# Reordering the first loads of an RNN and LSTM kernel: input weights first, x over two queues, h0 behind the bias rows

## The chip, the cores and the metric

The kernel runs on one core of a Trainium2 chip. The time is the device time of one execution in microseconds (us), given as the median of several runs. Engines: TensorE (PE; its weight loads are listed as PEld), VectorE (DVE), ScalarE (ACT), GpSimd (POOL) and SyncE (SP), which here only issues transfers. ACT issues a few transfers too; "SPq" and "ACTq" are the two engines' issuing instructions, and in the views of the DMA queues q1 is the queue of SP and q10 that of ACT.

## The reference

An RNN layer and an LSTM layer, each with a residual, over x of 32 sequences, 128 steps and 512 features, all float32:

```python
# x: (32, 128, 512); cond_1024: (32, 512); L0: Wx, Wh (512, 512), b (512); L1: Wx, Wh (512, 2048), b (2048)
def rnn(x, h0, Wx, Wh, b):
    xW = einsum('ntd,dh->nth', x, Wx) + b
    h = h0
    for t: h = tanh(h @ Wh + xW[:, t]);  h_t[:, t] = h
def lstm(x, h0, Wx, Wh, b):
    c = 0; h = h0
    for t: a = (x @ Wx + b)[:, t] + h @ Wh
           i, f, o = sigmoid(a[:, 0:H]), sigmoid(a[:, H:2H]), sigmoid(a[:, 2H:3H]);  g = tanh(a[:, 3H:])
           c = f * c + i * g;  h = o * tanh(c);  h_t[:, t] = h
x = x + rnn(x, cond_1024, ...)
x = x + lstm(x, cond_1024, ...)
```

## The kernel before

The kernel is one program with a hand-written stream for each engine, ordered by semaphores. A global step k runs from 0 to T + 6 (T = 128): at k the RNN does its step k and the LSTM its step k - 7. The hidden state of 32 sequences by 512 units lies on 128 partitions as four quarters of 32 (`quarter(j)`, j the block of 128 units). x comes in groups of four time steps (`TG`): `load_x` (L418) fetches one group by four transfers of 64 KB, one for each quarter j, all adding to one semaphore. Every 512 bytes of it is a separate row in memory.

All weights are fetched whole and stay on the chip: WxR and WhR (`wxr_raw`, `whr_raw`, 1 MB each), WhL and WxL (`whl_raw`, `wxl_raw`, four chunks of 1 MB each). The names `in_L_cond_Wx` and so on of the trace stand for both layers. SP issues x's group 0, WxR, WhR and then the chunks (L429 to L440); the helper `load_chunk` (L425) issues a chunk only when an earlier load has landed: the first chunk of WhL behind WxR, the second behind WhR, each later one behind the chunk two before it. ACT issues h0 and the two biases at its start (L603 to L606), then loads its function table (L610, by way of a small sigmoid).

What the first step needs, engine by engine:

- PE (from L1474): six warming matmuls on the identity (`fill`, L1470); the RNN bias spread to all partitions by a small product (L1479), which needs the bias rows `bias_rows_r` (they are landed in `pre_r`); the same into the two RNN banks (L1482); the LSTM bias product (L1484), which needs `bias_rows_l` (landed in `pre_l`); six more fills, which wait for ACT's copy of the RNN bias (`bias_done`, L614); `product_r(0)` (L1393), x times WxR; two fills; `recurrent_r(0)` (L1404), h0 times WhR.
- DVE (from L1154): `turn_x(0)` (L906), the transposition of x's group 0, which waits for its four quarters; `start_state` (L895, L896), two transpositions of h0, one for each layer; `rnn_weight_peak` (L1047), the largest absolute value of WxR; then `rnn_turn(0)` (L1152), the transposition of the first new state, which waits for ACT's tanh (L810).
- ACT: the bias copy (L614), tanh of step 0 (L810), and then `bias_of_l` (L618) and the peak of WhR (L729) before tanh of step 1.

```python
            for k in range(END):
                ...
                if k == 0:
                    fill(ps_pk, 2)
                if k < LAG:
                    recurrent_r(k)
```

Of the kernel before, what the change touches and what calls it, by code (L numbers as in the profile page):

```python
# [13 lines left out]
TG = 4  # L14
DMA = 16
# [26 lines left out]
def rnn_lstm_kernel(nc, x, h0, WxR, WhR, bR, WxL, WhL, bL, out):  # L42
    B, T, D = x.shape
    H = WhR.shape[0]
    J = H // P
# [7 lines left out]
    with ctx:  # L53
        def sb(name, shape, dt=F32):
            return ctx.enter_context(nc.sbuf_tensor(name, shape, dt))
# [4 lines left out]
        def sem(name):  # L60
            return ctx.enter_context(nc.semaphore(name))
# [20 lines left out]
        h0n = sb("h0n", [P, P])  # L82
# [84 lines left out]
        s_h0 = sem("h0_loaded")  # L167
# [201 lines left out]
        def wait(eng, s, value):  # L369
            if value > 0:  # L370
                eng.wait_ge(s, value)
# [15 lines left out]
        def sliced_dram(t, first):  # L387
            v = t.rearrange("b t (j u) -> j b t u", j=J)
            return [v[j, :, first:first + TG, :] for j in range(J)]

        def chunk_rows(w, k):
            return w.rearrange("(p k) n -> k p n", k=J)[k]
# [5 lines left out]
        def quarter(j):  # L398
            return slice(j * B, (j + 1) * B)
# [11 lines left out]
        def store_last(eng, j):  # L411

            done = stored if j < 2 else stored_by_act
            eng.dma_start(sliced_dram(out, T - TG)[j][:, TG - 1, :], xb[(NG - 1) % NX][quarter(j), TG - 1, :]).then_inc(done, DMA)

        block = ctx.enter_context(nc.Block())

        def load_x(eng, g):  # L418
            for j, src in enumerate(sliced_dram(x, g * TG)):
                eng.dma_start(xb[g % NX][quarter(j), :, :], src).then_inc(x_in[g % NX], DMA)  # L420

        @block.sync
        def _(sp):

            def load_chunk(dst, w, k, loaded, behind):  # L425
                sp.wait_ge(behind, DMA)
                sp.dma_start(dst, chunk_rows(w, k)).then_inc(loaded, DMA)

            load_x(sp, 0)  # L429
            sp.dma_start(wr_raw[OF_X][:, :], WxR.rearrange("(p k) n -> p (k n)", k=J)).then_inc(s_wr[OF_X], DMA)  # L430
            sp.dma_start(wr_raw[OF_H][:, :], WhR.rearrange("(p k) n -> p (k n)", k=J)).then_inc(s_wr[OF_H], DMA)
            load_chunk(whl_raw[0][:, :], WhL, 0, s_whl[0], s_wr[OF_X])
            load_chunk(whl_raw[1][:, :], WhL, 1, s_whl[1], s_wr[OF_H])
            load_x(sp, 1)
            load_chunk(whl_raw[2][:, :], WhL, 2, s_whl[2], s_whl[0])
            load_chunk(whl_raw[3][:, :], WhL, 3, s_whl[3], s_whl[1])
            load_chunk(wxl_raw[0][:, :], WxL, 0, s_wxl[0], s_whl[2])
            load_chunk(wxl_raw[1][:, :], WxL, 1, s_wxl[1], s_whl[3])
            load_chunk(wxl_raw[2][:, :], WxL, 2, s_wxl[2], s_wxl[0])
            load_chunk(wxl_raw[3][:, :], WxL, 3, s_wxl[3], s_wxl[1])  # L440
            load_x(sp, 2)
            sp.wait_ge(s_wxl[2], DMA)
            load_x(sp, 3)
            for g in range(4, NX):
                load_x(sp, g)
            def peaks_to_row(i):
                first, count = BATCHES[i]
                sp.wait_ge(x_peaked, first + count - G1)
                if i == BY_PRODUCT:
                    sp.wait_ge(t_split, 8)  # L450
                wait(sp, row_reduced, i - BY_PRODUCT)
                sp.dma_start(peak_row,
                             peaks[:, X_PEAK + first:X_PEAK + first + count]).then_inc(row_loaded, DMA)

            def peaks_to_all(i):
                n = i - BY_PRODUCT
                sp.wait_ge(row_reduced, n + 1)
                wait(sp, scale_step, X_STEPS * (i - 1) + 1 if n > 0 else 0)
                sp.dma_start(peak_wide, peak_largest.unsqueeze(1).broadcast_to([1, P, 4])).then_inc(wide_loaded, DMA)

            for g in range(NG - 1):

                if g in EXCHANGE_BEHIND:
                    peaks_to_row(EXCHANGE_BEHIND[g])
                    peaks_to_all(EXCHANGE_BEHIND[g])
                sp.wait_ge(out_done, TG * (g + 1))
                for j, dst in enumerate(sliced_dram(out, g * TG)):
                    sp.dma_start(dst, xb[g % NX][quarter(j), :, :]).then_inc(stored, DMA)
                if g + NX < NG:
                    sp.wait_ge(stored, DMA * J * (g + 1))  # L470
                    load_x(sp, g + NX)

            sp.wait_ge(out_done, T - 1)
            for j, dst in enumerate(sliced_dram(out, T - TG)):
                sp.dma_start(dst[:, 0:TG - 1, :], xb[(NG - 1) % NX][quarter(j), 0:TG - 1, :]).then_inc(stored, DMA)
            sp.wait_ge(out_done, T)
            for j in (0, 1):
                store_last(sp, j)
            sp.wait_ge(stored, DMA * (J * (NG + 1) - 2))
            sp.wait_ge(stored_by_act, 2 * DMA)  # L480
# [119 lines left out]

        @block.scalar
        def _(act):
            act.dma_start(h0n[:, :], h0.rearrange("b (j u) -> j b u", j=J)).then_inc(s_h0, DMA)  # L603
            act.dma_start(bias_rows_r, bR.rearrange("(j u) -> j u", j=J)).then_inc(s_bias_r, DMA)
            act.dma_start(bias_rows_l.rearrange("j (g u) -> j g u", g=G),
                          bL.rearrange("(g j u) -> j g u", g=G, j=J)).then_inc(s_bias_l, DMA)  # L606


            act.wait_ge(ones_done, 1)
# [277 lines left out]
        def _(dve):  # L887
# [162 lines left out]
            def rnn_weight_low(of):  # L1050
                dve.wait_ge(r_high[of], 3)
                for (dst, src), (high, _) in zip(r_parts(wr[of][1], wr_raw[of]), r_parts(wr[of][0], wr_raw[of])):
                    nc.vector.scalar_tensor_tensor(out=dst, in0=src, scalar=r_scale[:, of:of + 1],
                                                   in1=high, op0=ALU.mult, op1=ALU.subtract).then_inc(r_split, 1)
# [533 lines left out]
```

## Time and profile before

| | us |
|---|---|
| median of 3 runs | 849.19 |
| the runs | 849.07 to 853.11 |
| span of the profiled execution | 847.5 |
| PE busy | 830.7 (98%) |
| DVE busy | 660.3 (78%) |
| ACT busy | 582.7 (69%) |
| POOL busy | 337.6 (40%) |

The page gives for the profiled execution its span, from the first to the last instruction; its own time is not shown apart from that, and the median of the runs is 1.7 above the span. The busy time of PE is modelled from the starts of pipelined matmuls. The chain of waits is followed back from the last instruction: each piece is what the next was released by. In the views in order of time, rows that are alike are merged, and the bracket at a row's end is the idle time ahead of it on its engine and what ended it.

### The profile page before, as it was taken

The numbers are of one execution on the slowest core, as the hardware profiler recorded it, in microseconds if no ns is written. First come the engines' busy times: TensorE is split into PE (matmuls) and PEld (weight loads), VectorE is DVE, ScalarE is ACT, GpSimd is POOL, SyncE is SP. The second block draws the span as 40 slices with busy tenths as digits, with TensorE's granted clock in tenths as the row PEclk, the third lists the DMA queues.
The fourth block names the chain that finished last, engine by engine and source line by source line (L and its number), as shares of the span: only waits on it lengthen the run. The fifth ranks groups of instructions, "written<-read, shape, count | busy, mean of one in ns | idle before, by whom it ended". The sixth has DMA issues, their size and how long they took to land.

```text
span 847.5 us, 52211 instructions
## 1 busy us (share of the span) xinstructions
PE 830.7 (98%) x22860; PEld 621.8 (73%) x22860; DVE 660.3 (78%) x1830; ACT 582.7 (69%) x1596; POOL 337.6 (40%) x697
## 2 busy tenths in 40 slices
PE   7999999999999999999999999999999999999996
PEld 4665556687777877777777787777777777777885
DVE  3579688788887877888778887888878887777765
ACT  4896477777676777766767776676777677677642
POOL 1212466834334343443444434344343443434320
PEclk9999999999999999999999999999999999999999
DMA  8801100111001111100111100011110000000000
GB/s 319 267 19 27 29 15 16 28 29 29 17 17 30 29 29 29 29 10 23 29 29 29 29 21 20 22 29 29 29 28 17 17 17 17 17 15 17 16 15 18
DMA packets 40196, 30.71 MB, mean 36 GB/s; under 512 B 5772, under 2 KB 38688, under 8 KB 38688
## 3 DMA queue, kind: packets, MB, share of 16 engines
q1 hardware_dynamic: 39712, 27.27, 11.2%
q8 instruction: 179, 2.93, 1.5%
q14 instruction: 49, 0.40, 0.2%
q10 hardware_dynamic: 256, 0.11, 0.0%
HBM read 18.95 MB, written 8.39 MB: 32 GB/s over the span
## 4 chain that ended last, share of the span: by engine, by line
PE 93%; DVE 3%; ACT 2%; DMA 1%; issue 1%; SPq 0%; ACTq 0%; DVEq 0%
PE ps_l L1279 35%; PE ps_l L1345 28%; PE ps_r L1422 9%; PE ps_r L1442 9%; PE ps_l L1323 4%; PE ps_l L1292 2%; PE ps_l L1312 2%; PE ps_r L1404 1%; PE ps_r L1393 1%; DMA whr_raw<-in_L_cond_Wh 1%; PE ps_l L1238 1%; DVE pre_l L1080 0%; PE ps_l L1266 0%; ACT gates L795 0%; PE ps_l L1256 0%
## 5 line engine op out<-in xcount | busy, mean ns | idle before, releaser
L496 POOL TENSOR_TENSOR xb<-xb,h_l 128x128 f32<-128x128 f32 x127 | 58.0, 457 | 420.3 <-DVE h_lo L1126 414.2
L1345 PE MATMUL ps_l<-whl_raw,wxl_raw 128*32 128x256 f16 x3888 | 125.2, 273 | 1.7 <-ACT wxl_raw L700 1.3
L1345 PE MATMUL ps_l<-wxl_hi,wxl_raw 128*32 128x256 f16 x2592 | 124.6, 273 | 0.0
L1279 PE MATMUL ps_l<-whl_hi,hT_hi 128*32 128x512 f16 x1888 | 123.5, 379 | 1.1 <-DVE hT_hi L1110 1.1
L1279 PE MATMUL ps_l<-whl_hi,hT_lo 128*32 128x512 f16 x1888 | 123.3, 379 | 0.0
L1279 PE MATMUL ps_l<-whl_lo,hT_hi 128*32 128x512 f16 x1888 | 123.3, 379 | 0.0
L1345 PEld LDWEIGHTS ps_l<-whl_raw,wxl_raw 128*32 128x32 f16 x3888 | 104.0, 97 | 15.8 <-ACT ps_l L681 2.7
L795 ACT ACTIVATE gates<-pre_l 128x256 f32<-128x256 f32 x108 | 45.1, 417 | 101.5 <-DVE pre_l L1080 101.5
L1279 PEld LDWEIGHTS ps_l<-whl_hi,hT_lo 128*32 128x32 f16 x1888 | 51.9, 97 | 50.3
L1279 PEld LDWEIGHTS ps_l<-whl_lo,hT_hi 128*32 128x32 f16 x1888 | 51.9, 97 | 50.3
L1080 DVE SCALAR_TENSOR_TENSOR pre_l<-ps_l,g_products,wxl_raw 128x256 f32<-128x256 f32 x108 | 47.5, 480 | 48.3 <-PE ps_l L1279 43.6
L1080 DVE SCALAR_TENSOR_TENSOR pre_l<-ps_l,g_products,bias_l 128x256 f32<-128x256 f32 x108 | 47.5, 480 | 47.1 <-PE ps_l L1279 40.9
L533 POOL TENSOR_TENSOR whr_raw<-whr_raw 128x64 f32<-128x64 f32 x216 | 80.5, 393 | 4.2
L1345 PEld LDWEIGHTS ps_l<-wxl_hi,wxl_raw 128*32 128x32 f16 x2592 | 70.8, 97 | 12.0
L810 ACT ACTIVATE h_r<-pre_r 128x128 f32<-128x128 f32 x114 | 35.4, 310 | 63.8 <-DVE pre_r L1137 63.8
L1345 PE MATMUL ps_l<-wxl_lo,wxl_raw 128*32 128x256 f16 x1296 | 73.8, 273 | 0.0
L1279 PEld LDWEIGHTS ps_l<-whl_hi,hT_hi 128*32 128x32 f16 x1888 | 51.5, 97 | 27.3 <-DVE hT_hi L1110 1.4
L1152 DVE STREAM_TRANSPOSE hT_r<-h_r 128x128 f32<-128x128 f32 x128 | 52.7, 412 | 18.8 <-ACT h_r L810 18.7
L565 POOL TENSOR_TENSOR whr_raw<-xT,hT_r 128x128 f32<-128x128 f32 x108 | 50.0, 463 | 27.6 <-DVE hT_r L1152 27.6
L802 ACT ACTIVATE tanh_c<-c 128x128 f32<-128x128 f32 x128 | 39.5, 309 | 30.9 <-DVE c L1095 25.7
L747 ACT ACTIVATE xr<-ps_r,g_products 64x128 f32<-64x128 f32 x114 | 41.5, 364 | 26.4 <-PE ps_r L1422 21.6
L505 POOL TENSOR_TENSOR xb<-xb,h_r 128x128 f32<-128x128 f32 x128 | 59.4, 464 | 0.0
(178 smaller groups left out, 1936.4 us busy)
## 6 DMA issues: line engine op xcount, KB each, us to landing
xb<-in_x SPq DMA_DIRECT2D x128, 64.0 KB, 2.2
out<-xb SPq DMA_DIRECT2D x124, 64.0 KB, 1.8
whl_raw<-in_L_cond_Wh SPq DMA_DIRECT2D x4, 1024.0 KB, 6.4
wxl_raw<-in_L_cond_Wx SPq DMA_DIRECT2D x4, 1024.0 KB, 5.9
wxr_raw<-in_L_cond_Wx SPq DMA_DIRECT2D x1, 1024.0 KB, 5.6
whr_raw<-in_L_cond_Wh SPq DMA_DIRECT2D x1, 1024.0 KB, 7.7
out<-xb SPq DMA_DIRECT2D x4, 48.0 KB, 1.6
wxl_raw<-peaks SPq DMA_DIRECT2D x5, 2.0 KB, 1.9
```

Of the source, the lines that this page charges most:

```text
L496: nc.gpsimd.tensor_tensor(xb[g % NX][:, t, :], xb[g % NX][:, t, :], h_l[s % 2][:, :], ALU.add).then_inc(out_done, 1)
L505: nc.gpsimd.tensor_tensor(xb[g % NX][:, t, :], xb[g % NX][:, t, :], h_r[r % 2][:, :], ALU.add).then_inc(y_done, 1)
L533: nc.gpsimd.tensor_tensor(y[:, out, :, :], y[:, a, :, :], y[:, b, :, :], op).then_inc(y_blocks, 1)
L565: nc.gpsimd.tensor_tensor(yA[g % 2][:, first:first + 2, :, t // 2, :], xT[g % 2][:, :, t, :].rearrange("p (a k) b -> p a k b", a=2), hT_r[ ...
L747: nc.scalar.activation(xr[r % 2][0:64, :], ps_r[r % 2][64:128, P:2 * P], ACT.Copy, scale=unscale_r[64:128, g:g + 1])
L795: nc.scalar.activation(gates[:, 0:2 * P], pre_l[:, 0:2 * P], ACT.Sigmoid).then_inc(lstm_act, 1)
L1080: nc.vector.scalar_tensor_tensor(out=pre_l[:, half * HALF:(half + 1) * HALF], in0=gates_psum(s, half), scalar=unscale_l(s), in1=added[half ...
L1152: nc.vector.transpose(hT_r[:, :, :], by_chunk(h_r[r % 2][:, :])).then_inc(rnn_hT, 1)
L1279: last = nc.tensor.matmul(ps_l[s % 4][quarter(j), :], (hT_hi, hT_lo)[h_part][:, k, :], gate_slice(whl[w_part][k], j), start=False, stop=(h ...
L1345: last = nc.tensor.matmul(at[quarter(j), :], stationary, weights[:, j, :, :], start=False, stop=(y_part == 1 and k == 1), skip_group_check ...
L1422: last = nc.tensor.matmul(ps_r[r % 2][quarter(2 * p + c), 0:2 * P], (hT_r_hi, hT_r_lo)[h_part][:, 2 * p + k, :], quadrant_of_r16(wr[OF_H][ ...
L1442: last = nc.tensor.matmul(ps_r[r % 2][quarter(2 * p + c), 0:2 * P], x16[x_part][g % 2][:, 2 * p + k, t * B:(t + 1) * B], quadrant_of_r16(w ...
```

## The change

`load_x` gets an argument for the quarters it loads. SP's first transfer is WxR, then the quarters 2 and 3 of x's group 0, then WhR. ACT's first transfers are quarters 0 and 1, then the RNN bias rows, the LSTM bias rows, and h0. Nothing else differs; the line numbers of the new kernel are one higher behind L419 or two behind L603.

```diff
-        def load_x(eng, g):
-            for j, src in enumerate(sliced_dram(x, g * TG)):
+        def load_x(eng, g, quarters=range(J)):
+            for j in quarters:
+                src = sliced_dram(x, g * TG)[j]
                 eng.dma_start(xb[g % NX][quarter(j), :, :], src).then_inc(x_in[g % NX], DMA)
...
-            load_x(sp, 0)
             sp.dma_start(wr_raw[OF_X][:, :], WxR.rearrange("(p k) n -> p (k n)", k=J)).then_inc(s_wr[OF_X], DMA)
+            load_x(sp, 0, (2, 3))
             sp.dma_start(wr_raw[OF_H][:, :], WhR.rearrange("(p k) n -> p (k n)", k=J)).then_inc(s_wr[OF_H], DMA)
...
-            act.dma_start(h0n[:, :], h0.rearrange("b (j u) -> j b u", j=J)).then_inc(s_h0, DMA)
+            load_x(act, 0, (0, 1))
             act.dma_start(bias_rows_r, bR.rearrange("(j u) -> j u", j=J)).then_inc(s_bias_r, DMA)
             act.dma_start(bias_rows_l.rearrange("j (g u) -> j g u", g=G),
                           bL.rearrange("(g j u) -> j g u", g=G, j=J)).then_inc(s_bias_l, DMA)
+            act.dma_start(h0n[:, :], h0.rearrange("b (j u) -> j b u", j=J)).then_inc(s_h0, DMA)
```

SP's stream from its start, before (`wxr_raw` and `whr_raw` are WxR and WhR, `xb` is x):

```order
1 L420 DMA xb<-in_x 32x4x128 x4
2 L430 DMA wxr_raw<-in_L_cond_Wx 128x2048
3 L431 DMA whr_raw<-in_L_cond_Wh 128x2048
4 L427 DMA whl_raw<-in_L_cond_Wh 128x2048 [waits wxr_loaded]
5 L427 DMA whl_raw<-in_L_cond_Wh 128x2048 [waits whr_loaded]
```

and after the change:

```order
1 L430 DMA wxr_raw<-in_L_cond_Wx 128x2048
2 L421 DMA xb<-in_x 32x4x128 x2
3 L432 DMA whr_raw<-in_L_cond_Wh 128x2048
4 L428 DMA whl_raw<-in_L_cond_Wh 128x2048 [waits wxr_loaded]
5 L428 DMA whl_raw<-in_L_cond_Wh 128x2048 [waits whr_loaded]
```

WxR has moved ahead of x, and two of x's four quarters are gone from SP. ACT's stream from its start, before (`h0n` is h0, `pre_r` and `pre_l` are where the bias rows land):

```order
1 L603 DMA h0n<-in_cond 128x1x128
2 L604 DMA pre_r<-in_L_cond_b 4x128
3 L605 DMA pre_l<-in_L_cond_b 4x4x128
4 L610 ACT_TABLE_LOAD
5 L610 ACTIVATE table_first<-ones 128x1
```

and after the change:

```order
1 L421 DMA xb<-in_x 32x4x128 x2
2 L605 DMA pre_r<-in_L_cond_b 4x128
3 L606 DMA pre_l<-in_L_cond_b 4x4x128
4 L608 DMA h0n<-in_cond 128x1x128
5 L612 ACT_TABLE_LOAD
6 L612 ACTIVATE table_first<-ones 128x1
```

Two transfers of x stand ahead of the bias rows, h0 behind them, and the table load has two more issues in front of it less h0's earlier place.

## Rows read from the trace of the kernel before

**Rows 1.** The page: span, busy time of each engine, and the chain by engine.

```profile
span 847.5 us, 52211 instructions
...
PE 830.7 (98%) x22860; PEld 621.8 (73%) x22860; DVE 660.3 (78%) x1830; ACT 582.7 (69%) x1596; POOL 337.6 (40%) x697
...
PE 93%; DVE 3%; ACT 2%; DMA 1%; issue 1%; SPq 0%; ACTq 0%; DVEq 0%
```

**Rows 2.** The chain in order of time, 0 to 60 us: start us, us, what.

```profile
0.74 0.38 SPq L420
...
1.18 0.42 SPq L420
...
2.67 0.49 SPq L430
...
3.21 7.66 DMA whr_raw<-in_L_cond_Wh
...
10.91 1.12 PE ps_r L1404 x32
...
17.01 0.68 issue
...
23.30 0.77 issue
```

**Rows 3.** Rows in order of time, PE, 0 to 12 us: start, us, what [idle before].

```profile
1.52 2.74 PE L1470 MATMUL ps_l<-ident 128*128 128x512 f16 x6 [1.52 <-POOL ident L486]
...
4.65 0.46 PE L1479 MATMUL ps_l<-pre_r,gates 4*128 4x128 f32 x2 [0.39 <-DMA pre_r<-in_L_cond_b]
...
5.48 1.12 PE L1484 MATMUL ps_l<-pre_l,gates 4*128 4x512 f32 x2
...
6.54 1.47 PE L1470 MATMUL ps_l<-ident 128*128 128x512 f16 x6
...
8.31 1.08 PE L1393 MATMUL ps_r<-wxr_raw,xT 128*32 128x128 f32 x32 [0.31 <-DMA wxr_raw<-in_L_cond_Wx]
...
9.33 0.60 PE L1470 MATMUL ps_pk<-ident 128*128 128x512 f16 x2
...
10.91 1.08 PE L1404 MATMUL ps_r<-whr_raw,hT_r 128*32 128x128 f32 x32 [0.98 <-DMA whr_raw<-in_L_cond_Wh]
```

**Rows 4.** Rows in order of time, DVE, 5 to 13 us.

```profile
5.80 1.08 DVE L906 STREAM_TRANSPOSE xT<-xb 128x512 f32<-128x512 f32 x1 [3.98 <-DMA xb<-in_x]
...
6.82 0.35 DVE L895 STREAM_TRANSPOSE hT_r<-h0n 128x128 f32<-128x128 f32 x1
7.11 0.36 DVE L896 STREAM_TRANSPOSE h0T<-h0n 128x128 f32<-128x128 f32 x1
...
8.29 2.29 DVE L1047 TENSOR_REDUCE peaks<-wxr_raw 128x1 f32<-128x2048 f32 x1 [0.83 <-DMA wxr_raw<-in_L_cond_Wx]
...
12.37 0.42 DVE L1152 STREAM_TRANSPOSE hT_r<-h_r 128x128 f32<-128x128 f32 x1 [1.79 <-ACT h_r L810]
```

**Rows 5.** DMA issues of 0.7 to 1 us and of 0 to 4.4 us, last number us to landing.

```profile
xb<-in_x SPq DMA_DIRECT2D x1, 64.0 KB, 1.9
...
wxr_raw<-in_L_cond_Wx SPq DMA_DIRECT2D x1, 1024.0 KB, 5.6
```

**Rows 6.** Rows in order of time, ACT, 0 to 5 us.

```profile
0.75 1.17 ACTq L603 DMA_DIRECT2D h0n<-in_cond  x1
1.95 0.31 ACTq L604 DMA_DIRECT2D pre_r<-in_L_cond_b  x1
2.30 0.29 ACTq L605 DMA_DIRECT2D pre_l<-in_L_cond_b  x1
2.62 1.28 ACT L610 ACT_TABLE_LOAD   x1 [2.62 <-issue]
3.92 0.20 ACT L610 ACTIVATE table_first<-ones 128x1 f32<-128x1 f32 x1
```

**Rows 7.** DMA queues, 2.18 to 2.5 us, then 6 to 9 us: packets, MB, engines' share.

```profile
q1 hardware_dynamic: 42, 0.02, 20.6%
q10 hardware_dynamic: 29, 0.01, 15.2%
...
DMA packets 170, 1.26 MB, mean 421 GB/s; under 512 B 16, under 2 KB 16, under 8 KB 16
...
q1 hardware_dynamic: 170, 1.26, 100.3%
```

**Rows 8.** The last two WxL chunks: issue, the last one's landing time, its first weight load.

```profile
27.32 2.79 SPq L427 DMA_DIRECT2D wxl_raw<-in_L_cond_Wx  x2
...
wxl_raw<-in_L_cond_Wx SPq DMA_DIRECT2D x1, 1024.0 KB, 5.6
...
36.73 0.14 PEld L1246 LDWEIGHTS ps_l<-wxl_raw,yT 128*32 128x32 f32 x4
```

**Rows 9.** By stage: busy (x) of PE, PEld, DVE, ACT, POOL; granted clock, DMA share, GB/s.

```profile
0.00:4.30 4.30, 2.74 (x6) 0.73 (x6) 0.49 (x2) 1.49 (x2) 0.99 (x8) 1.00 0.41 96
```

## The prediction

> **What bounds the kernel now.** I read the page first: the span, the engines' shares and the chain that ended last [rows 1]. The reader should see that TensorE (PE) is busy 98% of the span and holds 93% of the chain; no operation of PE, VectorE (DVE), ScalarE (ACT) or GpSimd is changed here. Only the opening is touched, where the chain has 1% of DMA. So I read the chain in order of time next [rows 2]. It starts with SyncE issuing four quarters of the first x (0.74 to 2.63), then WxR (wxr_raw, 2.67), then WhR (whr_raw, 3.21), waits 7.66 us for WhR, and lets `recurrent_r(0)` start at 10.91. Call that start R. Behind R the chain in order of time has only PE, ACT, DVE and "issue" pieces, no DMA; the later weight loads have cover (below). So a microsecond won or lost at R is one at the end, if nothing else gives way.
>
> Third, what else must be there before R. PE's own rows in order of time [rows 3]: fills that need only the identity (1.52 to 4.26); the RNN bias product (4.65), started by the landing of the bias rows; the two ps_r products; the LSTM bias product (5.48 to 6.60); six fills (to 8.01); `product_r(0)` at 8.31, started by WxR; two fills (9.33 to 9.93); then 0.98 us of waiting for WhR. Two lengths follow: from the bias row's landing to the end of the six fills 8.01 - 4.65 = 3.36, and from `product_r(0)` to the end of the last fills 9.93 - 8.31 = 1.62. With B for the landing of bias_rows_r and no other wait, R cannot come before B + 4.98. With B at 4.65 that is 9.63: **PE's opening has 1.28 us of slack today.** DVE's rows [rows 4]: `turn_x(0)` at 5.80 when x has landed (1.08), `start_state` (0.35 and 0.36), then the peak of WxR (2.29, to 10.58), and `rnn_turn(0)` at 12.37, 1.46 behind R. It has 1.8 us of slack.
>
> **The change, part by part.**
>
> *WxR first on SyncE.* Its issue moves from 2.67 to 0.74. The trace has no WxR with nothing ahead of it. Upper end: today's 5.6 us from issue to landing [rows 5], so 6.3. Lower end: the first x quarter lands 1.9 us after its issue [rows 5], and one more megabyte costs the distance of the landings of WxR (PE started on it at 8.31) and WhR (10.91) [rows 3], 2.6 us: 0.74 + 1.9 + 2.6 = 5.2. I take the middle, 5.8. That no longer matters to `product_r(0)`, if PE's fills end later than that.
>
> *WhR's issue.* Two x issues fewer ahead of it, 0.38 and 0.42 [rows 2], with their gaps of 0.05: from 3.21 to about 2.3. Upper end with its 7.66: 9.95. Lower end: 2.6 behind WxR's 5.2, 7.8; with 0.5 for the two x quarters in between (four issues a step of 0.48, [rows 2]) 8.3. From the middle, 5.8 + 2.6 + 0.5 = 8.9. So **WhR comes 0.9 to 2.6 us earlier, and stops being what R waits for.** The chunks of WhL and WxL, each issued by the landing two before, come earlier with it; nothing in the chain waited for them, so I cost that at nothing. The cover: the second-last WxL chunks land before PE asks, and the last, issued last in the stretch that ends at 30.11 and 5.6 to landing, so there by 35.7, is a microsecond ahead of its weight load at 36.73 [rows 8].
>
> *Two x quarters on ACT ahead of the bias rows.* This is the price. ACT's issues now: h0 1.17, bias 0.31, bias 0.29 [rows 6]. I take the 1.17 for whatever comes first on ACT and 0.38 to 0.51 for a second x; the RNN bias is then issued at about 0.75 + 1.17 + 0.45 = 2.4 and not at 1.95. Lower end for B: the same 2.7 us from issue to landing as now (1.95 to 4.65) and 0.35 for the shortest extra issue, 5.0. The upper end comes from what stands ahead. An x quarter is 128 rows of 512 bytes, 8 for each of the 16 DMA engines; ACT's queue had one such transfer (h0) before the bias rows and now has two, and beside them SyncE's queue holds no longer other small rows but WxR. In the stretch where weights alone move, 154 packets over 512 bytes take 48.1 engine-microseconds (1.003 x 16 x 3), 0.31 each, carrying 8 KB [rows 7]. If the two queues take turns on an engine, each of ACT's first 8 small packets waits for one of WxR's 8, and the bias rows come behind the second x right after WxR: 5.2 to 6.3 plus up to 0.5 for a quarter, so 6.8 at the top. The trace has no row of small beside large packets to choose by; I take WxR's middle and 0.2 for the small rows behind it, which is also about the middle of the two ends: **B = 6.0.** Then R = 6.0 + 4.98 = 10.98 against 10.91: **+0.1 us.** With the ends, R is 10.0 (-0.9) to 11.8 (+0.9); WhR at 9.95 at the worst is under all of it.
>
> The Trainium skill, page "DMA: Bandwidth & Descriptors", section "Queues, rings and completion order", says that each DMA engine goes round its queues a packet at a time; that rule speaks against this change. The only mixing the trace shows, small with small (q1 and q10 both moving, [rows 7]), does not contradict it; no row here has small beside large. By strict turns the sum is the +0.1 above, with ACT's small rows passing freely it is -0.9. The same page, section "Issuing engines are not separate DMA queues", says that a second issuing engine saves only issue time; by that alone the gain is the 0.9 of WhR's issue.
>
> *The ACT table load* follows the last issue: from 2.62 it moves by two x issues less the reordered h0, about 0.9, to end with its first use at about 5.0 instead of 4.12 [rows 6]. The bias copy needs PE, at B + 0.5 = 6.5; hidden. If that cover were gone it would cost the difference, under 0.5.
>
> *h0 behind the bias rows.* Issued about 3.1 instead of 0.75. DVE needs it for hT_r. It takes turns with WhR's packets, so I put it at 9.2, between WhR's 8.9 and its 9.95. hT_r is then there at 9.6, under R. Behind it on DVE stand h0T (0.36) and the WxR peak (2.29), 9.2 + 0.35 + 0.36 + 2.29 = 12.2, against `rnn_turn(0)` wanted at 10.98 + 1.46 = 12.44. Cover 0.2; cost nothing.
>
> *x itself:* `turn_x(0)` ends before 8.5 even if x lands 1.5 later than at 5.8; PE wants it at B + 3.36 = 9.4. Nothing.
>
> **Sum:** +0.1 us. The profiled execution's span is 847.5; 847.5 + 0.1 = 847.6, and with the 1.7 by which the median of the runs (849.19) stands above that span, **849.3**. I call anything within 0.5% (4.2 us) no change, about what a measurement of this kernel can tell. Even the whole 1.28 of slack is a third of that.
>
> **The rivals.**
>
> 1. *The bias rows get through at once* (B = 5.0): R = 10.0, limited equally by B and WhR's upper end: 0.9 faster, 848.3. For it: a 512-byte packet is short, and the bias rows are few. Against: today's bias landing already takes 2.7 us behind one h0.
>
> 2. *h0 is what comes last.* Its 128 small rows take turns with WhR and WhL; at the worst it lands where WhR does now, 10.87. DVE then runs h0's two transposes and the WxR peak until 10.87 + 3.0 = 13.9 and `rnn_turn(0)` comes 1.5 late, the first step's recurrence behind it: 850.7. The point from which it decides is a landing after 9.4. For it: the cover I found is 0.2. Against: WhR's bytes should be through by then.
>
> 3. *PE's clock.* The six fills before 4.26 take 2.74 us, the six before 8.01 take 1.47 [rows 3], though the granted-clock column says 1.00 [rows 9]; by the durations PE was at first at the lower of its two levels (1.2 and 2.4 GHz) and later at the higher. The new wait before the bias product is 1.7 us and not 0.39. If that sets the level back, the fills cost 1.27 more and `product_r(0)` up to 1: about +2.3, 851.6. Against: the 0.98 of waiting before R did it no harm, the matmuls after it take as long as those ahead (1.08 for 32).
>
> 4. *It doesn't do what it says:* WxR's first bytes come no earlier because WxR shares with x from two queues, and all landings stay. Then R is held by WhR or B near where it is: no change, 849.2.
>
> **How the numbers follow.** Forecast (with rival 4, which gives the same time) 0.52; bias rows early 0.25; h0 late 0.18; clock 0.05. The cases span 848.3 to 851.6. One of the three runs was at 853.11, 3.9 above the median, so a median of few runs can stray upwards by more than the mechanism. The range leaves the clock case and the strays partly out: 847.5 to 851.6, the low end 0.8 under the fastest case because earlier weight chunks may shorten one of the two unexplained PE pauses (0.68 and 0.77, [rows 2]). None of the cases reaches 0.5%; only strays do: faster 0.02, same 0.94, slower 0.04.
>
> **What would show it.** SyncE: WxR issued at 0.74, WhR near 2.3. `product_r(0)` not started by a DMA but straight behind the fills, near 9.4. The wait before `recurrent_r(0)` gone or tiny, with R within 0.9 of 10.9. The bias product starting at 5.0 to 6.8 and named as waiting for pre_r; PE's idle time moved from in front of WhR to in front of the bias product. `rnn_turn(0)` started by ACT's h_r, not by DVE's own queue. The forecast is wrong if R moves by over 1 us, if a DMA again stands in front of R, or if R moves and the end does not follow it one for one.

## The result and the profile after

| | median, us | runs | lowest to highest |
|---|---|---|---|
| before | 850.22 | 22 | 849.00 to 853.11 |
| changed | 851.60 | 22 | 850.83 to 852.63 |

The ratio is 1.0016 with a 95% interval of 1.0008 to 1.0023: the changed kernel is 1.4 us slower, 0.16%, which is no change by the 0.5% of the prediction, and it is clear of the noise. The kernel before has spread out with more runs: its median is 1.0 above the one the prediction started from. A second series of the changed kernel (e12 below) gave 1.0014 (1.0003 to 1.0024).

The page of the changed kernel, span and chain by engine, against [rows 1]. The span is 1.9 us longer, and ACT's share of the chain has gone from 2% to 3%:

```profile
span 849.5 us, 52211 instructions
...
PE 93%; ACT 3%; DVE 2%; issue 1%; DMA 1%; ACTq 0%; DVEq 0%
```

The chain in order of time, 0 to 40 us (start, us, what), against [rows 2]. It no longer starts with SyncE and WhR but with ACT's queue and the RNN bias rows:

```profile
0.73 0.42 ACTq L421
...
1.67 5.26 DMA pre_r<-in_L_cond_b
```

PE's rows in order of time, against [rows 3]:

```profile
1.52 2.74 PE L1472 MATMUL ps_l<-ident 128*128 128x512 f16 x6 [1.52 <-POOL ident L487]
...
7.06 0.76 PE L1481 MATMUL ps_l<-pre_r,gates 4*128 4x128 f32 x2 [2.79 <-DMA pre_r<-in_L_cond_b]
...
8.47 1.91 PE L1486 MATMUL ps_l<-pre_l,gates 4*128 4x512 f32 x2
...
10.31 2.74 PE L1472 MATMUL ps_l<-ident 128*128 128x512 f16 x6
...
12.98 1.94 PE L1395 MATMUL ps_r<-wxr_raw,xT 128*32 128x128 f32 x32
...
14.85 1.03 PE L1472 MATMUL ps_pk<-ident 128*128 128x512 f16 x2
...
15.81 1.08 PE L1406 MATMUL ps_r<-whr_raw,hT_r 128*32 128x128 f32 x32
```

Two things are to be seen. The bias product starts at 7.06 and not at 4.65, after 2.79 us of waiting. And from there each group takes longer than it did: the six fills 2.74 instead of 1.47, `product_r(0)` 1.94 instead of 1.08, the two fills 1.03 instead of 0.60. These are the durations of the first fills at 1.52: PE works at the lower of its two levels (1.2 and 2.4 GHz) until just before `recurrent_r(0)`, which takes 1.08 as before. From the start of the bias product to R it is 8.75 us, and before it was 6.26, with 0.31 of waiting for WxR and 0.98 for WhR in it. R is at 15.81, **4.9 us later than before** (one profile of each kernel; a second profile of the changed kernel, e12, has R at 15.14).

DVE's rows, against [rows 4]:

```profile
7.26 1.08 DVE L908 STREAM_TRANSPOSE xT<-xb 128x512 f32<-128x512 f32 x1 [5.44 <-DMA xb<-in_x]
...
10.70 0.41 DVE L897 STREAM_TRANSPOSE hT_r<-h0n 128x128 f32<-128x128 f32 x1 [2.35 <-DMA h0n<-in_cond]
...
11.31 2.24 DVE L1049 TENSOR_REDUCE peaks<-wxr_raw 128x1 f32<-128x2048 f32 x1
```

x, h0 and the peak are all done by 13.6, ahead of R. The issues of SyncE and ACT, and the DMA issues with their time to landing, against [rows 5, 6]:

```profile
0.73 0.90 ACTq L421 DMA_DIRECT2D xb<-in_x  x2
0.74 0.39 SPq L430 DMA_DIRECT2D wxr_raw<-in_L_cond_Wx  x1
...
1.67 0.58 ACTq L605 DMA_DIRECT2D pre_r<-in_L_cond_b  x1
2.12 0.67 SPq L432 DMA_DIRECT2D whr_raw<-in_L_cond_Wh  x1
```

```profile
wxr_raw<-in_L_cond_Wx SPq DMA_DIRECT2D x1, 1024.0 KB, 5.5
whr_raw<-in_L_cond_Wh SPq DMA_DIRECT2D x1, 1024.0 KB, 7.7
```

The weights did what the change wanted: WxR landed at 6.2 and not 8.3, WhR at 9.8 and not 10.9. The RNN bias was issued earlier than before (1.67 against 1.95) and landed 2.3 later.

The DMA queues of the changed kernel from 3.0 to 3.5 and from 4.0 to 4.5 us show why:

```profile
DMA packets 41, 0.19 MB, mean 380 GB/s; under 512 B 0, under 2 KB 19, under 8 KB 19
...
q1 hardware_dynamic: 22, 0.18, 85.3%
q10 hardware_dynamic: 19, 0.01, 6.4%
...
q1 hardware_dynamic: 26, 0.21, 100.4%
q10 hardware_dynamic: 24, 0.01, 8.1%
```

22 packets of 8 KB on SyncE's queue beside 19 small ones on ACT's, then 26 beside 24: by these counts the two queues take turns about one for one in this profile (e3 and e1 below look otherwise). Before, from 2.18 to 2.5 us, ACT's queue moved 29 small packets in a third of a microsecond beside small ones [rows 7]; beside large ones it moves 24 in a half. By the Trainium skill, page "DMA: Bandwidth & Descriptors", section "Queues, rings and completion order", each DMA engine goes round its queues a packet at a time; this trace agrees, with the 19 beside 22 and 24 beside 26 above.

### The profile page after: what moved, and what is told of

It is laid out like the page before. It is cut to its first block, busy times and chain, and to the rows that moved or that the text cites. A ratio compares the mean times of both kernels' runs of the same rounds, so it can differ in the third digit from the quotient of the medians.

```text
span 849.5 us, 52211 instructions
## 1 busy us (share of the span) xinstructions
PE 832.7 (98%) x22860; PEld 621.1 (73%) x22860; DVE 661.0 (78%) x1830; ACT 582.0 (69%) x1596; POOL 339.0 (40%) x697
## 4 chain that ended last, share of the span: by engine, by line
PE 93%; ACT 3%; DVE 2%; issue 1%; DMA 1%; ACTq 0%; DVEq 0%
PE ps_l L1281 35%; PE ps_l L1347 28%; PE ps_r L1424 9%; PE ps_r L1444 9%; PE ps_l L1325 4%; PE ps_l L1294 2%; PE ps_l L1314 2%; PE ps_r L1395 1%; ACT whl_lo L714 1%; PE ps_r L1406 1%; DMA pre_r<-in_L_cond_b 1%; DVE pre_l L1082 0%; PE ps_l L1268 0%; PE ps_l L1258 0%; PE ps_l L1248 0%
## 5 line engine op out<-in xcount | busy, mean ns | idle before, releaser
L1347 PEld LDWEIGHTS ps_l<-whl_raw,wxl_raw 128*32 128x32 f16 x3888 | 104.0, 97 | 15.8 <-ACT ps_l L683 2.7
L506 POOL TENSOR_TENSOR xb<-xb,h_r 128x128 f32<-128x128 f32 x128 | 61.4, 480 | 0.0
```

The costliest lines, as they stand in the source:

```text
L506: nc.gpsimd.tensor_tensor(xb[g % NX][:, t, :], xb[g % NX][:, t, :], h_r[r % 2][:, :], ALU.add).then_inc(y_done, 1)
L1347: last = nc.tensor.matmul(at[quarter(j), :], stationary, weights[:, j, :, :], start=False, stop=(y_part == 1 and k == 1), skip_group_check ...
```

## The experiments

Two theories stood after this reading. **A:** the bias rows are late because they queue behind x on ACT beside WxR, PE has nothing to do for 2.8 us, and then works at its lower level. **B:** h0, which landed at 10.7 as rival 2 feared, would cost as much by itself. Each run has one profile, of one of its executions, while the ratios come from all of them. The experiments also had to say how 4.9 us at R became 1.4 to 1.9 at the end.

### e1: bias rows first on ACT

```diff
-            load_x(act, 0, (0, 1))
             act.dma_start(bias_rows_r, ...)
             act.dma_start(bias_rows_l..., ...)
+            load_x(act, 0, (0, 1))
             act.dma_start(h0n[:, :], ...)
```

> The change, with ACT's issues in the order bias rows, x quarters 0 and 1, h0. Theory A (the bias rows are late because they queue behind x beside WxR, PE idles 2.8 us and then works at its lower level until recurrent_r(0)): the bias rows land before 4.7, the second six fills take 1.47 and not 2.74, recurrent_r(0) starts at 10 to 11.3, and the end is 0 to 0.9 us under the kernel before. Theory B (h0's late landing, 10.7, is what costs): h0 is still behind two x quarters, so recurrent_r(0) still waits until 11.1 or later, DVE's queue (h0T, the peak of WxR to about 13.5) holds rnn_turn(0), and the end is 1 to 1.5 us over the kernel before.

852.08 against 849.87, ratio 1.0015 (1.0004 to 1.0025): nothing gained on the changed kernel. The RNN bias product started straight behind the first fills, but its rows show the lower level still, and the LSTM bias rows came only at 5.96 (order of time, PE and DVE):

```profile
4.19 0.79 PE L1481 MATMUL ps_l<-pre_r,gates 4*128 4x128 f32 x2
...
5.96 2.07 PE L1486 MATMUL ps_l<-pre_l,gates 4*128 4x512 f32 x2
...
7.96 2.74 PE L1472 MATMUL ps_l<-ident 128*128 128x512 f16 x6
9.17 1.09 DVE L908 STREAM_TRANSPOSE xT<-xb 128x512 f32<-128x512 f32 x1 [7.34 <-DMA xb<-in_x]
```

Theory A in its simple form falls: in this profile an early RNN bias did not by itself bring the higher level. x, now behind the bias rows, landed at 9.2, later than in the changed kernel. From 2 to 5 us ACT's queue moved no packet at all, though its x quarters were issued from 1.64 on; SyncE's moved 126. R was 13.46.

### e2: the change with more fills

```diff
             fill(ps_l[3], 3)
             fill(ps_l[0], 3)
+            fill(ps_l[3], 11)
             pe.wait_ge(spread_j_done, 1)
```

> The change, with 11 more fills on PE before the bias product (not needed for the result), so that PE works from 1.5 to about 7 us. It takes the idle stretch away and leaves the late landing. Theory A splits here: if the level of PE's clock is the larger part, the second six fills take 1.47 again, recurrent_r(0) starts 5.0 behind the bias rows' landing, at about 12 and not 15.8, and the end is within 0.5 us of the kernel before. If the idle stretch is not what sets the level back, the fills still take 2.74 and nothing moves. Theory B: recurrent_r(0) is at 12 as well, but rnn_turn(0) waits for DVE until 13.6, and the end stays 1 us or more over.

849.43 against 849.87, ratio 0.9997 (0.9988 to 1.0005). Adding 11 matmuls whose result is not used took away all that the change had cost. PE's rows:

```profile
1.52 6.78 PE L1472 MATMUL ps_l<-ident 128*128 128x512 f16 x17 [1.52 <-POOL ident L487]
...
8.23 0.48 PE L1482 MATMUL ps_l<-pre_r,gates 4*128 4x128 f32 x2
...
9.96 1.47 PE L1472 MATMUL ps_l<-ident 128*128 128x512 f16 x6
...
12.91 1.08 PE L1406 MATMUL ps_r<-whr_raw,hT_r 128*32 128x128 f32 x32
```

The second fills take 1.47 again, and from the bias product to R it is 12.91 - 8.23 = 4.68 us and not 8.75: **the level costs 4.1 us of the opening.** (In e12's profile of the changed kernel the same stretch is 7.97, and the cost 3.3.) In this profile R is still 2.0 later than before, h0 is as late as in the changed kernel (its transposition at 10.87), and yet the median is not later. The profiled execution itself is the slowest of e2's eleven, 851.25, with a span of 849.4; PE waits 0.99 us for a late WxL chunk in it. So its rows speak of the opening and not of the typical end. Theory B falls: h0's landing is hidden here, with 0.6 us of cover (DVE was done with the peak at 13.7 and `rnn_turn(0)` came at 14.36, released by ACT).

### e3: WxR first alone

```diff
-            load_x(sp, 0)
             sp.dma_start(wr_raw[OF_X][:, :], WxR...)
+            load_x(sp, 0)
             sp.dma_start(wr_raw[OF_H][:, :], WhR...)
```

(against the kernel before; ACT's issues are untouched).

> One part of the change alone: SyncE issues WxR, then all four x quarters, then WhR; ACT issues h0 and the bias rows as before. Taking turns: h0's eight small packets an engine wait for WxR's eight, so the bias rows, behind them, land at 5.5 to 6.5 although ACT's queue is as before; PE idles 1.3 to 2.2 us before the bias product. Rival (ACT's small packets pass freely and only the second x transfer ahead of the bias rows delays them): the bias rows land at 4.6 as before and recurrent_r(0) starts near 10.

852.84 (5 runs) against 849.87, ratio 1.0035 (1.0022 to 1.0049), the worst of the orders. ACT's queue is as before, with h0 alone ahead of the bias rows, and still they landed 4 us later than before:

```profile
8.61 0.76 PE L1480 MATMUL ps_l<-pre_r,gates 4*128 4x128 f32 x2 [4.35 <-DMA pre_r<-in_L_cond_b]
```

So WxR at the head of SyncE's queue is enough to delay them, without a second x transfer on ACT. But it is not done by turns here. From 2 to 5 us the only queue with packets is SyncE's, although h0 was issued on ACT at 0.74:

```profile
DMA packets 140, 0.93 MB, mean 309 GB/s; under 512 B 8, under 2 KB 28, under 8 KB 28
...
q1 hardware_dynamic: 140, 0.93, 77.4%
```

ACT's queue moved its first packet just before 5.1 us, when 126 of WxR's 128 had gone. The same holds in e1. Why its rows got turns from 2.5 us on in the changed kernel and none in these two is not shown. By stages, this run also shows the level itself; columns are the stretch, its length, busy (x) of PE, PEld, DVE, ACT and POOL, granted clock, DMA share and GB/s:

```profile
7.00:10.00 3.00, 1.39 (x6) 1.42 (x7) 0.94 (x1) 0.28 (x1) 0.00 (x0) 0.72 1.02 344
10.00:13.00 3.00, 3.00 (x7) 0.79 (x6) 2.89 (x4) 0.00 (x0) 0.00 (x0) 0.50 0.94 333
13.00:16.00 3.00, 3.00 (x37) 1.45 (x36) 0.00 (x0) 0.00 (x0) 0.00 (x0) 0.65 1.00 356
```

0.50 is the 1.2 GHz level. PE did nothing from 4.26 to 8.61; the clock fell in the stretch from 7 to 10 and was back by 16.

### e4: small rows first

```diff
-            sp.dma_start(wr_raw[OF_X][:, :], WxR...)
             load_x(sp, 0, (2, 3))
+            sp.dma_start(wr_raw[OF_X][:, :], WxR...)
...
-            load_x(act, 0, (0, 1))
             act.dma_start(bias_rows_r, ...)
             act.dma_start(bias_rows_l..., ...)
+            load_x(act, 0, (0, 1))
             act.dma_start(h0n[:, :], ...)
```

> SyncE issues x quarters 2 and 3, then WxR, WhR; ACT the bias rows, x quarters 0 and 1, h0. x is still split over two queues, but no large packet is ahead of it. By taking turns: the bias rows land at about 3.5, WxR is issued about 0.9 earlier than before and WhR lands at about 10, recurrent_r(0) starts at 9.9 to 10.2, 0.7 to 1 us earlier than before, if h0 (behind x on ACT, beside WxR) lands before 9. The end is 0.3 to 1 us under the kernel before. Rival: the opening is absorbed further on by ACT's queue (which runs without a gap from the first tanh), and the end does not move by more than 0.3.

850.18 against 849.87, ratio 1.0004 (0.9993 to 1.0014). R did not come earlier but at 12.99: two x quarters on ACT behind the bias rows met WxR after all, and PE waited 3.19 us for x:

```profile
10.86 1.24 PE L1395 MATMUL ps_r<-wxr_raw,xT 128*32 128x128 f32 x32 [3.19 <-DVE xT L908]
```

The wait cost more than its length: the products behind it fell back to the lower level, and `recurrent_r(0)` took 1.94 instead of 1.08. Although R was 2.1 later than before, the first cell of the LSTM (tanh_c of step 7) was 0.2 later, and the end within the noise.

### e5: x over two queues, then WxR

```diff
-            sp.dma_start(wr_raw[OF_X][:, :], WxR...)
             load_x(sp, 0, (2, 3))
+            sp.dma_start(wr_raw[OF_X][:, :], WxR...)
```

(ACT as in the change).

> The change with WxR put back behind x on SyncE (x quarters 2 and 3, WxR, WhR; ACT as changed: x quarters 0 and 1, bias rows, h0). All of x travels with small rows only. Expected by taking turns: x landed by 4.5, the bias rows at 4.2 to 5.2 (only the last of them meet WxR's first packets), WhR about 10, no long idle stretch of PE, recurrent_r(0) at 10 to 10.5. If a start R that is 0.5 to 0.9 earlier is worth as much at the end, the kernel is 0.5 to 0.9 us faster than before; if the opening has play behind it (e4: R 2.1 late, step 7 only 0.2 late), 0 to 0.3.

851.62 (6 runs) against 849.34, ratio 1.0026 (1.0012 to 1.0040). x landed by 4.4, the RNN bias by 4.2 and WhR at 9.8, as expected. But the LSTM bias product began only at 7.18, after 1.3 us of idle PE, and PE was at the lower level before that wait and stayed there (the RNN bias products took 0.79 and 1.06, the six fills from 9.18 to 11.92); R was 14.49. So the idle stretch, R and the end came out wrong: even this order leaves the LSTM bias rows beside WxR, and the opening is lost to the level.

### e6: h0 behind the bias rows, alone

```diff
-            act.dma_start(h0n[:, :], ...)
             act.dma_start(bias_rows_r, ...)
             act.dma_start(bias_rows_l..., ...)
+            act.dma_start(h0n[:, :], ...)
```

(the kernel before otherwise).

> The third part of the change alone: the kernel before with h0 issued behind the bias rows on ACT. The bias rows land near 3 to 4 instead of 4.65, the bias products start right behind the first fills at 4.2, h0 lands by 6 to 8 beside WxR, WhR at 10.9 still sets recurrent_r(0): no change (within 0.5 us). Rival: PE's waits move (a longer one before product_r(0)), the clock level comes later or falls in some runs, and the median is 0.5 us or more over.

849.85 against 849.34, ratio 1.0012 (1.0002 to 1.0022): 0.5 to 1.0 over, the rival's side. In its profile PE was again at the lower level until 12 (R 12.55), and this without any wait: from 1.52 to 12.0 it was never idle.

```profile
7.48 2.74 PE L1471 MATMUL ps_l<-ident 128*128 128x512 f16 x6
10.15 1.94 PE L1394 MATMUL ps_r<-wxr_raw,xT 128*32 128x128 f32 x32
```

So an opening without a gap is no guarantee of the higher level. The weights were late too. WxR landed at 10.0 and not 8.3, and PE waited twice for a WxL chunk, for which the prediction had counted on a microsecond of cover:

```profile
35.58 1.07 PE L1247 MATMUL ps_l<-wxl_raw,yT 128*32 128x512 f32 x8 [1.50 <-DMA wxl_raw<-in_L_cond_Wx]
...
38.94 1.07 PE L1247 MATMUL ps_l<-wxl_raw,yT 128*32 128x512 f32 x8 [0.57 <-DMA wxl_raw<-in_L_cond_Wx]
```

### e7 and e8: only R late

```diff
                 if k == 0:
-                    fill(ps_pk, 2)
+                    fill(ps_pk, 16)
```

(29 in e8; the kernel before otherwise).

> The kernel before with 14 more fills (0.22 us each, not needed for the result) just ahead of recurrent_r(0): loads and clock as before, R later by 9.93 + 3.05 - 10.91 = about 2.1 us. If R counts one for one, the end is 2.1 later. If there is play of 2.7 us between R and step 7 (as in the changed kernel, where 4.9 at R became 2.2), the end does not move.

> The same with 27 more fills: R at 9.93 + 5.9 = 15.8, as late as in the changed kernel, but with the loads of the kernel before and PE at its higher level. If lateness of R is all that the change costs, the end is 1.4 to 2.2 us later, as in the changed kernel; if the changed order of the loads costs something by itself, it is less than that; if R counts one for one, 4.9.

e7: 852.84 against 849.34, ratio 1.0053 (1.0037 to 1.0068); e8: 854.58, 1.0063 (1.0051 to 1.0075). R was not where I had set it in either profile: loads and program are those of the kernel before up to the fills, and still the opening was partly (e8) or wholly (e7) at the lower level. The kernel before can therefore have a slow opening as well; its one profile, with R at 10.91, shows a good one. e7's six runs reach from 851.25 to 856.45, and its profile is the slowest of them:

```profile
16.01 1.08 PE L1404 MATMUL ps_r<-whr_raw,hT_r 128*32 128x128 f32 x32
...
23.35 0.66 PE L1404 MATMUL ps_r<-whr_raw,hT_r 128*32 128x128 f32 x8 [1.68 <-issue]
48.40 0.31 ACT L802 ACTIVATE tanh_c<-c 128x128 f32<-128x128 f32 x1 [0.56 <-DVE c L1095]
```

R is as late as in the changed kernel (5.1 against 4.9 later than before), with the loads in their old order, and the first cell is 6.9 later: more than R, not less. A pause of PE of 1.68 us that waits for nothing on record stands in between. e8's profile, order of time and then by stage:

```profile
6.38 1.55 PE L1470 MATMUL ps_l<-ident 128*128 128x512 f16 x6
8.74 1.94 PE L1393 MATMUL ps_r<-wxr_raw,xT 128*32 128x128 f32 x32 [0.81 <-DMA wxr_raw<-in_L_cond_Wx]
10.61 8.32 PE L1470 MATMUL ps_pk<-ident 128*128 128x512 f16 x29
18.86 1.08 PE L1404 MATMUL ps_r<-whr_raw,hT_r 128*32 128x128 f32 x32
```

```profile
7.60:7.80 0.20, 0.20 (x2) 0.00 (x0) 0.00 (x0) 0.00 (x0) 0.00 (x0) 0.60 1.18 492
```

The clock rose for the first products and was lost again between 7.6 and 7.8, while PE was still in its fills. The wait of 0.81 us for WxR came behind the fall and cannot have caused it; the idle time ahead of it is 0.42 us before 4.69. R was 18.86, 7.95 later than before, and the first cell 5.23 later (below): 2.7 us fewer between R and the first cell, the same as in the changed kernel, with the loads in their old order. So e8 lost 2.7 us of R's lateness on the way and e7 added 1.8 to it; neither sum belongs to the change. In the runs of e8 the end is 5.2 later, as its first cell says.

The start of tanh_c of step 7 in the kernel before, the changed kernel, e2 and e8:

```profile
41.50 0.31 ACT L802 ACTIVATE tanh_c<-c 128x128 f32<-128x128 f32 x1 [0.56 <-DVE c L1095]
```

```profile
43.69 0.31 ACT L804 ACTIVATE tanh_c<-c 128x128 f32<-128x128 f32 x1 [0.56 <-DVE c L1097]
```

```profile
41.90 0.31 ACT L804 ACTIVATE tanh_c<-c 128x128 f32<-128x128 f32 x1 [0.56 <-DVE c L1097]
```

```profile
46.73 0.31 ACT L802 ACTIVATE tanh_c<-c 128x128 f32<-128x128 f32 x1 [0.56 <-DVE c L1095]
```

### e9 to e12: the same fills elsewhere, and the change once more

e9 is the kernel before with e2's line, e10 is e1 with it, e11 is e5 with it; e12 is the changed kernel unaltered.

```diff
             fill(ps_l[0], 3)
+            fill(ps_l[3], 11)
```

> The kernel before with the same 11 more fills on PE ahead of the bias product. Its loads are as before. PE works from 1.5 to about 6.7 us, so its clock should be at the higher level by the bias product in every execution; recurrent_r(0) comes at about 11.7 instead of 10.9, which the play behind it should swallow. If the level in the opening is also what spreads the runs of the kernel before, its median falls by 0.3 to 0.8 us and few runs stand above 851. Rival: the spread has another cause (a late weight chunk), and median and spread stay.

> The order of e1 (bias rows ahead of the x quarters on ACT, WxR first on SyncE) with the 11 more fills. If e1's 1.3 us over was the clock level, it comes down to the kernel before or up to 0.5 under it; if it was x's and h0's late landing, it stays 1 us or more over.

> The order of e5 (x over two queues, then WxR) with the 11 more fills. As e10: level theory, from 2.2 over down to the kernel before or up to 0.5 under it; a late LSTM bias landing (7.2 in e5) alone would leave 0.5 or more over.

> The changed kernel once more, beside the others on one chip: 1.0 to 2.2 us over the kernel before, no run under 850.5.

| | median (before 849.88) | ratio, 95% interval | the same order without the fills |
|---|---|---|---|
| e9 | 850.35 | 1.0009 (0.9998 to 1.0020) | 1 |
| e10 | 849.99 | 1.0008 (0.9998 to 1.0018) | e1: 1.0015 (1.0004 to 1.0025) |
| e11 | 849.86 | 0.9997 (0.9989 to 1.0006) | e5: 1.0026 (1.0012 to 1.0040) |
| e12 | 851.36 | 1.0014 (1.0003 to 1.0024) | |

e12 repeats the change's loss. e11 gives back all of e5's, and its interval does not meet e5's; e10's gain on e1 is within the intervals. e9 fell for the rival: with the clock at its higher level (in its profile) the kernel before is no faster, and its runs still reach from 848.10 to 852.97. So the opening's level is not what spreads the runs of the kernel before, or not alone. A late weight chunk is another source: PE waits 1.0 to 2.1 us in all for WxL in the profiles of e2, e6 and e9, and there the span ends 807.4 to 807.8 us behind the first cell; in the other eleven profiles it is 805.6 to 806.4. No run here sets its share. No version beats the kernel before: e2 and e11 equal it, and the intervals of e4, e9 and e10 reach it.

e12's profile has the fall of the clock on record, which the first profile of the changed kernel has not:

```profile
4.30:7.00 2.70, 0.00 (x0) 0.00 (x0) 0.00 (x0) 0.43 (x2) 0.00 (x0) 1.00 1.09 370
7.00:10.00 3.00, 2.83 (x9) 1.17 (x10) 1.10 (x1) 0.28 (x1) 0.00 (x0) 0.71 1.05 385
```

Here PE was idle from 4.26 to 7.17, the RNN bias product behind the wait still ran at the higher level (0.46), and the clock fell between 8.1 and 8.4, a microsecond after PE had gone back to work. In the first profile of the changed kernel the same product takes 0.76: there the level was already low behind the wait. The six fills take 2.74 in both.

## Why the prediction was right, and where it was not

The measured 851.60 lies at the very top of the range, and the likeliest case, +0.1, did not happen. The case that did, the clock, I had given 0.05; that its 851.6 is the measured figure is luck, as its parts show below. By the prediction's own signs it failed: R moved by 4.9 us and not by less than 1, and the end did not follow one for one. Point by point:

- **The bound.** R waited for WhR before, and PE's opening had 1.28 us of slack: right, and the changed chain starts where the slack ran out, at the bias rows.
- **WxR and WhR.** 5.8 and 8.9 in the sum; 6.2 and 9.8 measured, inside both pairs of ends. WhR stopped being what R waits for, as said.
- **The bias rows.** B = 6.0 with a top of 6.8; PE started on them at 7.06, after a wait to 6.92. The mechanism, turns one for one with WxR, fits this profile, though e1 and e3 show that it is no rule. Two terms were short: WxR landed at 6.2 and not 5.8, and the bias rows 0.7 behind it, where I had 0.2. By 5.0 us ACT's queue had moved 109 of its 256 packets of x; the second quarter and the bias rows came after WxR, with the small rows of both queues.
- **ACT's issues.** I took 1.17 us for the first transfer whatever it was. x's first took 0.42 [a row of the chain above]; the 1.17 belonged to h0 coming first. A small error to the good.
- **PE's clock (rival 3).** This is the step that failed. I priced it at 2.3 us in all and gave it 0.05, because 0.98 us of waiting before R had done no harm. It cost 4.1 us in the opening (e2), as every group from the bias product on ran at the lower level. The two groups that I had priced, the six fills and `product_r(0)`, cost 1.27 and 0.86, near my 2.3; the bias products cost 1.52 and the last two fills 0.42, which I had at nothing. And the level need not be "set back" by the wait: in the first profile of the changed kernel it had not risen when the bias product came.
- **R counts one for one at the end.** Wrong, and it saved the range. R went up by 4.9, the first cell by 2.19, the last cell's tanh by 1.94, the median by 1.4. The 2.7 us between R and step 7 went in steps: `rnn_turn(2)` was still 4.90 late, `rnn_turn(3)` 4.16, `rnn_turn(4)` 3.40. That is two steps of about 0.75, at the two pauses of PE of 0.68 and 0.77 in [rows 2], which the changed kernel's profile does not have. A third, on PE's weight loads, stands a little further on in the kernel before:

```profile
30.22 0.14 PEld L1238 LDWEIGHTS ps_l<-whl_raw,h0T 128*32 128x32 f32 x3 [1.04 <-issue]
```

  and in the changed kernel the same eight matmuls run through without it (32.24, 1.09 us). 0.68, 0.77 and 1.04 are 2.5 of the 2.7. Lateness alone does not take these pauses away. From R to the first cell it is 27.9 us in the changed kernel, e3 and e8, where PE has no such pause; 30.6 in the kernel before; and 32.4 in e7, with R at 16.0. PE pauses for nothing on record in seven of the fourteen profiles, among them e1 (1.5), e5 (1.5 and 0.5) and e7 (1.7), whose R is 2.5 to 5.1 later than before. So the 2.7 is a difference between two single executions, and the 4.9 is one too: e7 shows that the old order of loads can have the low level as well. What the medians say is the 1.4.

  What the pauses are is open. In the kernel before, the queue that the page calls "instruction" moves one packet at 15.2, 21.4 and 27.7 us, each 1.5 to 1.9 us ahead of a pause (in e7 at 21.0, the pause beginning at 21.7). The changed kernel has such packets at 18.6, 24.4 and 29.9 and no pause behind them. That PE waits for instructions there is a guess that no run tests.
- **h0 (rival 2).** It landed at 10.7 against my 9.2, behind the 9.4 from which I had said it decides. That point was reckoned for R at 10.98. R at 15.8 covered it, and so did R at 12.9 in e2. What so late an h0 costs when R is early shows in e10: PE waited 0.46 us for its transposition before `recurrent_r(0)` and 0.72 for `rnn_turn(0)` after it.
- **x.** Landed 1.5 later than before, at 7.26, just the bound I had allowed; hidden.
- **The low end.** I had thought earlier chunks might shorten PE's pauses. They are gone in the changed kernel's profile, but e1 and e5 have the chunks early too and pause for 1.5 us. And the cover of the last WxL chunk, a microsecond in the one profile I had, was not there in e2, e6 and e9.

That the range held 851.6 is luck: it comes from two errors of opposite sign, 5 us at R and the 2.7 behind it, and to a median of the kernel before that moved up by 1.0.

## What to carry to other kernels

A few small transfers that an opening waits for should not be in flight beside a megabyte on another queue. In the changed kernel each packet of 8 KB took its 0.31 us [rows 7] ahead of the next small one, and in e3, and for x in e1, the small rows stood behind nearly the whole megabyte. When a wait grows in front of TensorE in an opening, price every instruction behind it at the lower level, up to the point where the level is known to be back, and not the wait alone; filling the wait with matmuls that are not needed won back here all that the change had lost. And do not count a start one for one at the end from a single profile of each kernel: with the same loads, R to the first cell was 27.9 us in one execution and 32.4 in another.

## What the runs showed of the hardware

- The level of PE's clock in the opening is not a fixed thing. With the same six fills from 1.52 to 4.26, the bias product right behind them ran at the lower level in e1, e5 and e6, and the level was still low at 10 us or later, with PE idle not at all (e6), 0.1 (e1) or 1.3 us (e5) in between. In the kernel before the same product, behind an idle 0.39 us, ran at the higher level. What decides it no run here shows. In all four profiles with the 11 fills (e2, e9, e10, e11) the level was high at the bias product.
- The fall of the clock need not come in the wait. In e12 it fell a microsecond after PE had gone back to work, in e8 during the fills, with an idle 0.42 us three microseconds earlier; in e4 PE was idle from 7.67 to 10.86, and the clock fell between 11.5 and 12.
- The granted-clock column misses switches: in the changed kernel's first profile it reads 1.00 in every stretch up to 20 us (as for 0 to 4.3 in [rows 9]), while the six fills at 10.31 take 2.74. The duration of a known matmul tells the level where the column does not: 0.42 or 0.22 us a fill.
- Rows of two queues do not always take turns. In the changed kernel ACT's small rows moved one for one with WxR's; in e1 and e3 none of them moved from 2 to 5 us, while WxR did.
- x landed later than before (5.8) in each order with WxR at the head of SyncE's queue: 7.3 in the changed kernel, 9.2 in e1, 9.1 in e3 (all of it on SyncE). Over two queues and ahead of WxR, in e5, it had landed by 4.4.
